# A conv, attention and expert-MLP block on one core: another written order of its stages

## What is computed

```python
# conv block, input x (16, 64, 16, 16)
h = silu(conv1x1(group_norm(x, 32), w0, b0))
h = silu(conv3x3(group_norm(h, 16), w1, b1, groups=4))     # 128 channels = 64 x radix 2
y = group_norm(h, 2)
a = y.mean(over 8x8 windows).max(over radix)
a = group_norm(silu(conv1x1(a, w2, b2, groups=2)), 8)
a = softmax(conv1x1(a, w3, b3, groups=2), over radix)
x = x + group_norm(einsum(y, a, weight), 32)
# causal attention over the image index t = 0..15, for each of 256 pixels, 64 channels
t = tokens(x); H = layer_norm(t)
e = tanh(H @ fc_w.T + fc_b) @ score_w
t = t + C     # C[t] = sum_{s<=t} softmax_{s<=t}(e[s]) * H[s], an online softmax scan
# 8 experts, dense, mixed by weights w that depend on the pixel alone
u = layer_norm(t); w = softmax(mean_t(u) @ Wr + br)
h1 = relu(bn(u @ W1[e])); h2 = relu(bn(h1 @ W2[e])); y = h2 @ Wo[e] + bo[e]
out = t + sum_e w[e] * y[e]
```

## Time and profile before

| what | value |
|---|---|
| time, three runs | 154.56, 155.56, 156.14 us (median 155.56) |
| the profiled execution | 154.75 us, span 152.8 us |
| TensorE busy | 129.6 us (85%), of it 8.0 us `heat` and 9.8 us `warm` products |
| VectorE, ScalarE, GpSimd busy | 102.1, 78.0, 31.0 us |
| granted TensorE clock, mean | 0.944 |

### The profile page before, as it was taken

The page is one execution under the profiler, slowest core; times in us unless marked ns, Lnnn a source line. Parts: engine busy times, 40 slices in busy tenths (PEclk is TensorE's granted clock), DMA queues, the critical chain, the costliest instruction groups (busy, mean ns, idle before and its releaser), DMA issues.

```text
span 152.8 us, 2584 instructions
## 1 busy us (share of the span) xinstructions
PE 129.6 (85%) x951; PEld 58.6 (38%) x953; DVE 102.1 (67%) x305; ACT 78.0 (51%) x162; POOL 31.0 (20%) x28
## 2 busy tenths in 40 slices
...
DMA packets 3835, 4.95 MB, mean 32 GB/s; under 512 B 240, under 2 KB 3440, under 8 KB 3696
## 3 DMA queue, kind: packets, MB, share of 16 engines
...
q10 hardware_dynamic: 144, 0.20, 0.6%
...
HBM read 3.75 MB, written 1.05 MB: 31 GB/s over the span
## 4 chain that ended last, share of the span: by engine, by line
PE 60%; DVE 24%; ACT 6%; POOL 5%; issue 4%; POOLq 0%
PE bank L1043 10%; PE bank L883 8%; PE bank L1016 8%; PE bank L1029 7%; DVE ctxs L713 4%; PE bank L831 3%; PE bank L933 2%; PE bank L895 2%; PE bank L900 2%; DVE y L651 2%; PE bank L925 2%; PE bank L838 2%; PE bank L814 2%; ACT y L380 1%; DVE s_wst L596 1%
## 5 line engine op out<-in xcount | busy, mean ns | idle before, releaser
L439 ACT ACTIVATE h<-bank,s_bnb 128x512 f32<-128x512 f32 x22 | 14.5, 691 | 10.0 <-PE bank L1016 10.0
L883 PE MATMUL bank<-pad,w 32*64 32x512 f32 x288 | 17.7, 595 | 0.2 <-DVE pad L554 0.2
L1016 PE MATMUL bank<-xs,f1s 64*64 64x512 f32 x128 | 17.1, 605 | 0.3 <-issue 0.2
L1029 PE MATMUL bank<-h,f2s 64*64 64x512 f32 x128 | 17.1, 603 | 0.3 <-ACT more L447 0.2
L831 PE MATMUL bank<-warm 128*128 128x512 bf16 x32 | 9.8, 464 | 1.3 <-POOL warm L323 1.3
L883 PEld LDWEIGHTS bank<-pad,w 32*64 32x64 f32 x288 | 6.8, 130 | 8.7 <-issue 7.8
L349 ACT ACTIVATE act<-bank,par 128x512 f32<-128x512 f32 x4 | 2.8, 689 | 13.1 <-PE bank L844 13.0
L738 DVE TENSOR_SCALAR h<-bank,s_bnb 128x512 f32<-128x512 f32 x10 | 7.5, 749 | 2.8 <-PE bank L1016 2.8
L955 PE MATMUL bank<-ctxs,par 128*128 128x128 f32 x32 | 6.6, 334 | 2.3 <-DVE ctxs L713 2.3
L838 PE MATMUL bank<-warm 128*128 128x512 bf16 x26 | 8.0, 440 | 0.3 <-issue 0.2
L895 PE MATMUL bank<-y,par 128*64 128x512 f32 x16 | 6.3, 928 | 2.0 <-DVE y L651 2.0
...
## 6 DMA issues: line engine op xcount, KB each, us to landing
...
```

Of the source, the lines that this page charges most:

```text
L439: A.activation(h1[(2 * m + h) % 4][:], bank[Z1[h]][:], ACT.Relu, bias=tile("bnb", P, 3 * EP)[:, col:col + 1]).then_inc(h1_ready, 1)
L883: ins = T.matmul(bank[CONV1[k][2 * j + h]][at:at + C, :], w1[rows, tap, :], pad[rows, b:b + 2, dy:dy + S, dx:dx + S], start=(tap == 0), st ...
L1016: ins = T.matmul(bank[Z1[h]][to, :], f1s[own, e, to], xs[own, k, q], start=True, stop=True)
L1029: ins = T.matmul(bank[Z2[h]][at:at + C, :], f2s[rows, h, e, :], h1[(2 * m + h) % 4][rows, :], start=True, stop=True)
```

## The change

Only the list is written anew. Each stage keeps its code, banks and buffers; nine of the fourteen `heat` stages are dropped (18 products of TensorE), and `SMALL_AT` and its like follow the new list. Two lines of it, each first as it was and then as it is:

```diff
-    silu.3 gn2.1 conv.5 conv.6 gn2f.1 conv.7 norm0.1 ws.0 ws.1 ws.2 ws.3 conv.8 ynorm.0 s1row.0 conv.9 silu.4 silu.5 conv.10 conv.11
-    s2row.0 conv.12 gn3.0 conv.13 conv.14 gn3f.0 silu.6 win.0 conv.15 conv.16 conv.17 ws.4 w2.0 ws.5 silu.7 ws.6 gna.0 gnaf.0 ws.7 gn3.1
...
+    conv.16 conv.17 silu.4 gn3.0 silu.5 ws.4 silu.6 gn3f.0 silu.7 ws.5 ws.6 ws.7 win.0 gn3.1 gn3f.1 w2.0 ynorm.0 gna.0 gnaf.0 ynorm.1
+    win.1 w2.1 wan.0 ynorm.2 gna.1 gnaf.1 gate.0 w3.0 wan.1 heat.0 heat.1 heat.2 gate.1 gate.2 gate.3 w3.1 outp.0 outp.1 gn4.0 gn4.1
```

More of the change, by code:

```diff
@@ L73 @@
-    wan.0 gn3f.1 gate.0 ynorm.1 gate.1 w3.0 win.1 outp.0 gn4.0 gn4f.0 heat.0 heat.1 ynorm.2 x1.0 heat.2 w2.1 heat.3 ln1.0 heat.4 tok.0
-    heat.5 heat.6 gna.1 heat.7 heat.8 ln1.1 ynorm.3 hn.0 heat.9 hn.1 hch.0 hch.1 fc.0 fc.1 coef.0 score.0 att.0 cen.0 heat.10 heat.11
-    heat.12 gnaf.1 scan.0 wan.1 cen.1 ln2.0 w3.1 heat.13 gate.2 gate.3 ln2.1 outp.1 xn2.0 xt.0 gn4.1 xn2.1 l1.0 gn4f.1 d1.0 xt.1 x1.1 t2.0
-    l1.1 l2.0 tok.1 d1.1 xr.0 ln1.2 d1.2 ln1.3 l1.2 l2.1 l1.3 d1.3 xr.1 hn.2 hn.3 d1.4 l2.2 l1.4 hch.2 hch.3 t2.1 fc.2 fc.3 score.1 coef.1
@@ L77 @@
-    l2.3 cen.2 cen.3 att.1 scan.1 d1.5 l2.4 l1.5 ln2.2 t2.2 d1.6 xn2.2 ln2.3 d1.7 xr.2 d1.8 l1.6 xn2.3 l2.5 l1.7 d1.9 xt.2 l2.6 l1.8 t2.3
-    xr.3 l2.7 l1.9 xt.3 l2.8 l1.10 logits.0 l2.9 l1.11 wt.0 l2.10 wb.0 wb.1 l1.12 l2.11 mix.0 mix.1 mix.2 mix.3 l1.13 l2.12 mix.4 mix.5
-    mix.6 mix.7 mix.8 mix.9 l1.14 l2.13 mix.10 mix.11 mix.12 mix.13 mix.14 mix.15 mix.16 mix.17 l1.15 l2.14 mix.18 mix.19 mix.20 mix.21
-    mix.22 mix.23 finish.0 l2.15 mix.24 mix.25 mix.26 finish.1 mix.27 mix.28 mix.29 mix.30 mix.31 finish.2 finish.3
+    warm.0 warm.1 warm.2 warm.3 warm.4 silu0.0 warm.5 gn1.0 gn1f.0 warm.6 silu0.1 warm.7 warm.8 warm.9 spr.0 gn1.1 warm.10 xnorm.0 warm.11
@@ new lines @@
+    gn4f.0 ynorm.3 heat.3 gn4f.1 x1.0 x1.1 ln1.0 ln1.1 s1row.0 ln1.2 heat.4 tok.0 hn.0 tok.1 s2row.0 hn.1 ln1.3 hch.0 hch.1 hn.2 fc.0 fc.1
+    hn.3 score.0 coef.0 cen.0 hch.2 hch.3 att.0 cen.1 fc.2 scan.0 fc.3 ln2.0 t2.0 ln2.1 score.1 coef.1 xn2.0 att.1 xn2.1 d1.0 cen.2 scan.1
+    d1.1 t2.1 xt.0 cen.3 l1.0 xt.1 l1.1 l2.0 d1.2 ln2.2 l1.2 xr.0 l2.1 ln2.3 l1.3 l2.2 d1.3 xr.1 t2.2 l1.4 xn2.2 d1.4 xn2.3 l2.3 xt.2 l1.5
+    d1.5 l2.4 xt.3 l1.6 xr.2 xr.3 d1.6 l2.5 logits.0 d1.7 l1.7 l2.6 t2.3 l1.8 l2.7 d1.8 wt.0 l1.9 l2.8 l1.10 wb.0 wb.1 d1.9 l2.9 l1.11
```

7 lines of the change are left out of this document (5 added, 2 removed).

## The result

The changed kernel takes 149.62 us (median of 4 runs, 148.92 to 149.83) where the kernel before takes 155.70 us beside it (4 runs, 154.56 to 156.14). The ratio is 0.9623, 95% interval 0.9586 to 0.966: faster by 3.8%. The forecast was 153.2 us in a range from 149.9 to 157.1. It is where rival 3 put it (149.9), though only in part by what rival 3 said.

What follows compares the result with a forecast made beforehand. A chain of short steps bounds the kernel up to the first expert product, TensorE after it. Last `mix` 3.3 us earlier plus 0.9 for the clock gives -2.4: 152.35 profiled, 153.2 us as median, range 149.9 to 157.1.

Steps and rivals of the forecast that it cites:

- rival 3: Expert layers: the second scan is fully covered (2.4 us less) and the clock holds (0.9 less); 149.9 us, chance 0.12.
- What bounds the kernel now: Whole kernel: a chain of short steps on other engines until the first expert product at 84.08, TensorE for 65.40 us after.
- The convolution: 1.8 us won: Convolution: removing s1row gives nothing, s2row 1.06 us, gn3.0 with its drain 0.5 to 0.7; it ends 1.75 us earlier.
- The window network: 4.2 us late: From gn3.1's sum to the first w3's tanh: half 0's network waits behind gn3.1, so the tanh moves from 46.40 to 50.65.
- Gate to residual: 7.0 us late: From w3's tanh to gn4.0's shift: ynorm.3 queues, both halves' statistics go first; the shift moves from 55.56 to 62.55.
- Attention to the first expert product: 5.9 us late: From gn4.0's shift through attention, both halves together: the first expert product moves from 84.08 to 90.0.
- What is left for TensorE then: From first expert product to last `mix`: 9.8 us of attention work moves ahead, new stalls come; 56.2 us instead of 65.4.
- My walk: Expert stretch: stepping through the duos one by one with every relu gave 55.1 us in all.
- my sum: Expert stretch: 55.6 us left, plus stalls of 2.4 and 0.45, less 1.1 of old waits, gave 57.3 us.
- The unknown: the clock between 70 and 77: Attention stretch with dropped `heat`: a low clock there may cost 0 to 1.7 us; 0.9 was taken.
- Rival 1: Attention: the clock stays low through fc, score and cen of both halves, some 7.5 us; result 159.8 us, chance 0.13.
- Rival 2: Chain from 42.0 to 90.0: some 45 hand-overs each 0.05 us dearer use up the gain; about 155.5 us, chance 0.23.

Runs made afterwards that it cites:

- two_waits: Changed kernel with ynorm.3 ahead of the second w3 tanh on ScalarE and half of duo 1's relu moved from VectorE to ScalarE; 149.36 us, ratio 0.960.
- apart_warm: Changed kernel up to gn4, then the old order with the halves apart, s1row and s2row spread out, three `heat` stages added around gn4; 161.09 us, ratio 1.037.
- rows_back: Changed kernel with s1row and s2row both put back into the convolution; 153.42 us, ratio 0.9835.
- s1row_back: Changed kernel with s1row alone put back into the convolution, in front of tap 9; 150.40 us, ratio 0.9671.
- best: Changed kernel plus three `heat` stages around gn4, seven between convolution and first w3, and ynorm.3 ahead of the second w3 tanh; 148.34 us, ratio 0.9536.

## Why the prediction was wrong in size

Against the profiled execution the forecast was 152.35, and it took 149.83: 2.52 us too much. This splits by the milestones into 1.08 at the first expert product (90.0 against 88.92), 0.57 in what is left for TensorE (56.2 against 55.63) and 0.9 for the clock. Another 1.02 us is not of the kernel: the profiled execution of before lay 0.81 below the median that the prediction used, that of after 0.21 above its own, and I had shifted by the first alone. Point by point:

- **What bounds the kernel now**: right. Two regimes, a chain up to the first expert product and TensorE from there. In eleven of the thirteen profiles the execution's time is the end of the last `mix` and 5.27 or 5.28 us more (two_waits 5.45, apart_warm 5.83).
- **The convolution: 1.8 us won**: the step that failed first, by a term that was too small. The last tap ended where it was forecast (gn3.0's product at 36.08, forecast 36.3) and s1row was free. But s2row was put down at 1.06 us, its price on TensorE, and ScalarE's silus were to "follow at their old pace". Taking s2row out of the taps moves the first silu of half 1 by 1.98 us (rows_back and s1row_back): in the kernel after it starts 0.71 us ahead of gn3.0's product, where in the kernel before it started 0.14 behind w2.0's (38.23 and 38.09), with ynorm.0 on ScalarE just in front of it. These 0.85 us were in no term. With 0.26 us by which this execution's convolution started earlier (17.79 against 18.05) they make the 1.0 us by which gn3.1's sum is early (40.99 against 42.0).
- **The window network: 4.2 us late**: right. From gn3.1's sum to the tanh of w3 it is 8.54 us, forecast 8.65.
- **Gate to residual: 7.0 us late**: right in mechanism, 0.5 us too long (11.44 us from tanh to shift, forecast 11.9). The wait for ynorm.3 is there.
- **Attention to the first expert product: 5.9 us late**: from 62.55 to 90.0 the forecast was 27.45 us, and measured are 27.95. That is made of two errors. It is 26.84 or 26.85 in five profiles of the merged order in which `tok` runs at full clock, 0.6 less than I walked (0.5 of it behind the context scan: 9.02 us from there, forecast 9.5); `tok` at low clock added 1.1 in this execution. The prediction had no low clock there. The four differences (1.01 and 0.11 and 0.46 early, 0.50 late) are the 1.08 us at the first expert product.
- **What is left for TensorE then**: the subtraction alone was right to 0.1 us: 65.4 - 9.8 = 55.6, and every kernel of the merged order but two_waits has 55.56 to 55.63. The stall of 2.4 us for d1.1 is the second term that was mis-sized. It measured 0.42, since the second scan starts only 2.0 us behind the first expert product (90.96) and TensorE has layer 1 of duo 1, layer 2 of duo 0 and ln2.2 to lay beside it, up to 94.52. The waits taken together are 1.11 us, fewer than the 1.40 of before. My walk (55.1) was nearer than my sum (57.3), and the middle of the two was 0.6 us off.
- **The unknown: the clock between 70 and 77**: the cost of 0.9 did not come there (1.00 in 69.90 to 73.70). It came, with almost the same size, between 59 and 66, or in the other profile as 1.0 us at outp; that the size fits is luck, as the place is another. So the 18 products dropped did matter, at another place: three stages put back at gn4 take 1.1 us off the chain (0.4 to 0.6% of the time). The Trainium skill, in TensorE: Matmul & The Clock Gate (section What's actually happening), says that activity releases the throttled state, and that the point at which the clock rises varies from run to run, which it measured at the start of a kernel. By the first the sum would have taken the full 1.7 us in this stretch, and the trace has none of it there. The second agrees with the two profiles of one program (outp 3.02 and 1.08 us in the one, 6.41 in the other).
- **Rival 3** named the number and half of the cause: the cover of the scan was nearly complete (2.0 of its 2.4 us), and the clock held where the 0.9 us were put. That its number fits is luck. It takes the whole 2.4 us off 56.2, which is the middle of a sum that has them and a walk that ended at 55.1. Full cover in that sum gives 55.6 + 0.45 - 1.1 = 54.95, the middle with the walk is 55.0, and the rival's time would be 153.2 - 1.2 - 0.9 = 151.1. The 0.85 us of the silus and the 1 us of the medians, which helped to bring the time down to 149.62, it does not name. **Rival 1** (the clock low through fc, score and cen) did not happen in the kernel after; rows_back is a mild form of it: fc.0 and fc.1 took 3.40 us there, 1.43 more than their 1.97 in the kernel after, and the chain 2.0 more. (Its price of 7.5 us is not what its words add up to: with all four terms for both halves it is 2 x (1.96 + 1.85 + 1.94) = 11.5. No run reaches either.) **Rival 2** (45 hand-overs each a little dearer) did not happen: whole segments moved as whole segments (squares to hn.1 4.87 us, as forecast, hn.1 to the first score scan 5.10, forecast 5.09).
- **The range** was cut off at rival 3's own number, with nothing for its causes coming together with the median's own offset of 1 us. That is why it missed by 0.28.

What stays open: why the second low place moves between executions (nothing here sets it), whether gn3.0's product among the taps would take the lead away by itself (every kernel with it there has ynorm.0 in front of the silus as well), what half 0 alone takes in an order with neither rows nor low clock in its way (the 26.03 us are an estimate), and whether `best` is faster than the kernel after by more than the noise.
